# A fused decoder block on one core: the identity products of two rounds taken out of TensorE's order

## The reference, cut to what matters

```python
x = x + L0_attn(layernorm(x), ...)          # gated delta rule: per head a 16 x 16 state,
                                            #   Sd = g * S;  S = Sd + k (beta * (v - k Sd));  o = q S
x = x + L0_xattn(layernorm(x), ctx, ctx)    # differential cross attention over 64 context rows
x = x + L0_ffn(layernorm(x), ...)           # causal convolution, 8 experts (top 2), small GELU block
```

## Time and profile before

| | us |
|---|---|
| three runs, median | 1509.95 |
| lowest, highest | 1508.57, 1512.37 |
| the profiled execution | 1508.25 |
| its span, first to last instruction | 1506.5 |

### The profile page before, as it was taken

How to read it: one execution, slowest core, us unless ns; L and a number is a source line. 1 busy time by engine, 2 the same in 40 slices (tenths; PEclk the granted TensorE clock), 3 DMA queues, 4 the chain that set the end, 5 groups by cost and what they waited for, 6 DMA issues and landing times.

```text
span 1506.5 us, 38146 instructions
## 1 busy us (share of the span) xinstructions
PE 1429.3 (95%) x15790; PEld 945.8 (63%) x15790; DVE 1187.0 (79%) x3205; ACT 834.3 (55%) x1599; POOL 205.5 (14%) x212
## 2 busy tenths in 40 slices
PE   5988899999999999999999999999999989899899
PEld 3654666655766566656766567655766557756765
DVE  7457978978887878977897888977898778966663
ACT  2555365646655565655756566655656455534453
POOL 0121211102301022002301023002201022001000
PEclk7999999999999999999999999999999999999999
DMA  6010010000100001000100001000100001000000
GB/s 236 1 29 30 2 29 22 10 1 15 30 29 2 2 18 26 30 2 2 43 30 2 2 15 29 30 1 2 44 15 3 1 16 30 16 2 15 1 1 15
DMA packets 20212, 31.27 MB, mean 21 GB/s; under 512 B 1480, under 2 KB 17864, under 8 KB 19784
## 3 DMA queue, kind: packets, MB, share of 16 engines
q1 hardware_dynamic: 20040, 28.82, 6.6%
HBM read 20.41 MB, written 8.39 MB: 19 GB/s over the span
## 4 chain that ended last, share of the span: by engine, by line
PE 80%; DVE 11%; ACT 6%; issue 2%; POOL 0%; DVEq 0%; ACTq 0%
PE bank L2116 15%; PE bank L2054 7%; PE bank L1808 7%; PE bank L1678 6%; PE four L1899 4%; PE bank L2039 4%; PE bank L2017 4%; PE bank L1703 3%; PE bank L1811 3%; PE four L1967 3%; PE four L1951 2%; PE four L1703 2%; PE bank L1684 2%; PE bank L1710 2%; PE four L1918 2%
## 5 line engine op out<-in xcount | busy, mean ns | idle before, releaser
L2116 PE MATMUL bank<-w_sb,cs 128*128 128x512 f32 x512 | 245.2, 597 | 0.3 <-ACT cs L1032 0.3
L739 POOL TENSOR_TENSOR decayed<-state,pk 128x512 f32<-128x512 f32 x64 | 67.7, 1058 | 842.0 <-DVE state L1414 842.0
L2116 PEld LDWEIGHTS bank<-w_sb,cs 128*128 128x128 f32 x512 | 94.6, 190 | 91.2 <-issue 83.4
L1032 ACT ACTIVATE cs<-bank 128x512 f32<-128x512 f32 x112 | 66.7, 595 | 148.8 <-PE bank L1684 126.2
L2054 PEld LDWEIGHTS bank<-vx_sb,cs 128*128 128x128 f32 x896 | 109.2, 190 | 25.9 <-ACT cs L982 16.6
L2054 PE MATMUL bank<-vx_sb,cs 128*128 128x136 f32 x896 | 119.9, 285 | 3.6 <-ACT cs L982 1.5
L982 ACT COPY cs<-bank 128x512 f32<-128x512 f32 x114 | 66.5, 583 | 95.3 <-PE bank L2039 95.3
L1808 PE MATMUL bank<-hT,w_sb 128*128 128x512 f32 (+1 forms) x224 | 109.4, 611 | 2.7 <-ACT rota L835 0.8
L1626 DVE SCALAR_TENSOR_TENSOR cs<-cs,rwt 128x256 f32<-128x256 f32 x196 | 88.7, 501 | 23.5 <-ACT cs L1032 22.4
L1273 DVE SCALAR_TENSOR_TENSOR qkv<-pre,l_sb,qkv 128x512 f32<-128x512 f32 x144 | 99.4, 746 | 0.2
L1498 DVE TENSOR_REDUCE pkc<-bank 128x8 f32<-128x512 f32 x116 | 75.0, 681 | 20.3 <-PE bank L2017 20.3
(11 more groups left out here) (283 smaller groups left out, 3015.7 us busy)
## 6 DMA issues: line engine op xcount, KB each, us to landing
xt<-in_x SPq DMA_DIRECT2D x8, 512.0 KB, 4.8
vscr<-qkv SPq DMA_DIRECT2D x8, 512.0 KB, 2.6
vT<-vscr SPq DMA_DIRECT2D x32, 128.0 KB, 4.4
Tm<-in_x SPq DMA_DIRECT2D x8, 512.0 KB, 3.8
out<-cs SPq DMA_DIRECT2D x8, 512.0 KB, 2.9
w_sb<-in_weights SPq DMA_DIRECT2D x1, 3656.0 KB, 18.1
w_sb<-in_weights SPq DMA_DIRECT2D x1, 1456.0 KB, 8.3
cs<-in_scratch SPq DMA_DIRECT2D x3, 256.0 KB, 8.6
```

The source lines that it names most:

```text
L2116: mm(dst, x1T[:, k, b * TB:b * TB + TB], ew[:, k, ep * 512:ep * 512 + 512], start=k == 0, stop=False)
```

## The change

The entries of KEEP for round 0 and for round NI - 1 are deleted: 51 products of round 0 and 44 of round 7, 95 of the 235. With the number 0, keep issues nothing and waits for nothing. Every other product of this kind stays, and so do all other instructions of all five engines, in the same order. The table's text gets six lines shorter, so that a line of the changed kernel has a number lower by six than the same line before.

```diff
-        20): 2, (-1, -1, "moe", 21): 6, (-1, -1, "moe", 3): 6, (-1, -1, "moe", 7): 1, (-1, 0, "co", 4, 0): 9,
-        (-1, 0, "cs", 4, 1): 1, (-1, 0, "raw", 2): 6, (-1, 1, "db"): 2, (0, -1, "moe", 19): 2, (0, -1, "moe",
-        22): 6, (0, -1, "moe", 30): 1, (0, -1, "sc", 6, 0): 8, (0, -1, "turn5", 1): 10, (0, 0, "co", 4, 1): 2,
-        (0, 0, "vturn"): 11, (0, 1, "proj", 1, 0): 1, (0, 2, "turn1", 0): 5, (0, 2, "turn1", 1): 5, (1, 0, "co",
-        1, 1): 3, (1, 0, "z", 3): 9, (NI - 1, -1, "pt", 5): 5, (NI - 1, -1, "pt", 6): 2, (NI - 1, -1, "pt", 7):
-        3, (NI - 1, -1, "pt", 9): 3, (NI - 1, -1, "pv", 1, 0): 3, (NI - 1, -1, "pv", 4, 0): 3, (NI - 1, -1,
-        "turn3", 1): 3, (NI - 1, 0, "co", 3, 0): 1, (NI - 1, 0, "co", 5, 1): 1, (NI - 1, 0, "sum", 2): 5, (NI -
-        1, 0, "wo", 1): 14, (NI - 1, 1, "gate", 1): 1, (NI, -1, "moe", 3): 1, (NI, -1, "pw", 0, 0): 17, (NI, -1,
-        "pw", 0, 1): 1, (NI, -1, "sc", 1, 0): 4, (NI, -1, "turn2", 0): 1, (NI, 0, "cs", 5, 1): 8, (NI, 0, "d1",
-        5): 9, (NI, 0, "decay"): 17, (-2, -1, "ffd", 1): 23, (-2, -1, "moe", 28): 3, (-2, -1, "pt", 6): 3, (-2,
-        -1, "pw", 0, 0): 7, (-2, -1, "sc", 1, 0): 11, (-2, -1, "turn6", 0): 4, (-2, 0, "co", 4, 1): 7, (-2, 0,
-        "cs", 6, 1): 6, (-2, 0, "raw", 1): 5, (-2, 2, "turn1", 0): 16}
+        20): 2, (-1, -1, "moe", 21): 6, (-1, -1, "moe", 3): 6, (-1, -1, "moe", 7): 1, (-1, 0, "co", 4, 0): 9, (-1, 0,
+        "cs", 4, 1): 1, (-1, 0, "raw", 2): 6, (-1, 1, "db"): 2, (1, 0, "co", 1, 1): 3, (1, 0, "z", 3): 9, (NI, -1,
+        "moe", 3): 1, (NI, -1, "pw", 0, 0): 17, (NI, -1, "pw", 0, 1): 1, (NI, -1, "sc", 1, 0): 4, (NI, -1, "turn2", 0):
+        1, (NI, 0, "cs", 5, 1): 8, (NI, 0, "d1", 5): 9, (NI, 0, "decay"): 17, (-2, -1, "ffd", 1): 23, (-2, -1, "moe",
+        28): 3, (-2, -1, "pt", 6): 3, (-2, -1, "pw", 0, 0): 7, (-2, -1, "sc", 1, 0): 11, (-2, -1, "turn6", 0): 4, (-2,
+        0, "co", 4, 1): 7, (-2, 0, "cs", 6, 1): 6, (-2, 0, "raw", 1): 5, (-2, 2, "turn1", 0): 16}
```

## The result

| | before | changed |
|---|---|---|
| median of 6 runs each, us | 1508.05 | 1522.61 |
| lowest, highest | 1504.37, 1512.37 | 1520.27, 1526.71 |
| the profiled execution | 1508.25 | 1520.27 |
| its span | 1506.5 | 1518.4 |
| its mean granted clock | 0.991 | 0.976 |

The changed kernel takes 1.0087 times as long, 95% interval 1.0065 to 1.011, 13.1 us more by the ratio (the plain medians are 14.6 apart). The forecast was slower by 5.8 us, 1515.8 with a range of 1509 to 1521. The sign is right; the size is less than half of what was measured, and the median lies 1.6 us above the range.

What follows compares the result with a forecast made beforehand. PE looked like the bound at 95% busy, but other engines pace the removed groups, so TensorE's clock decides. Clock-fall terms sum to 8.9 us; 0.7 of that, 6.2, less 0.4 gained gives +5.8: 1515.8 us, range 1509 to 1521.

Steps and rivals of the forecast that it cites:

- The 95 products give nothing back: Both rounds: of 21.2 us of PE time removed, only 0.4 us is gained, since other engines set the pace.
- in the way: Rival: a third of 64 exposed products delay the step behind them, so removal gains 4.8 us, 1505.2; chance 0.06.
- 96 to 100: Round 0: a clock fall slows vturn and cond behind it, 0.6 us (0 to 1.7).
- 119 to 123: Round 0: a clock fall slows the next projection, with ACT right behind it, 1.3 us (0 to 1.7).
- 167 to 182: End of round 0: two more falls behind the one at 171, mostly hidden by DVE, 1.0 us (0 to 3.4).
- Three pairs of pt and pv: Round 7 (1268, 1275, 1282): a fall doubles pv, whose DVE reader follows; 1.3 each, 3.9 us (0 to 5.1).
- behind other work: Rival: the clock falls, but DVE has other work first, so only +2.2 us, 1512.2; chance 0.14.
- The thinner groups at 1233, 1263, 1315: Round 7: falls at these smaller groups cost 0.4 us together (0 to 3.4).
- Ahead of wo: Round 7: a fall doubles part of wo's 3.68 us and DVE waits, 1.7 us (0 to 1.7).
- wo's 16 records still take less than 4 us: Round 7, sign that the forecast is wrong; it expected about 5.4 us instead of 3.7.
- taking 0.7 of it: Whole sum: 8.9 us cut to 6.2 for stretches where the clock holds, as at 1221.
- rival of the standing PE: Only gaps leaving PE idle over 3 us, ahead of vturn and wo, lose the clock: +1.9 us, 1511.9; chance 0.18.

Runs made afterwards that it cites:

- e11: Kernel before without 11 products of round 7 (turn3, co, sum, gate): 1513.31 us against 1508.83, 1.0024.
- e5: Kernel before without the 31 products at the end of round 0: 1511.84 us, ratio 1.0016, not told from no change.
- e6: Kernel before without the first 20 products of round 0: 1511.46 us, ratio 1.0006, not told from no change.
- e8: Kernel before without the 14 products ahead of wo in round 7: 1511.38 us, ratio 1.0013, not told from no change.
- e9: The changed kernel itself measured again, all 95 products gone: 1520.34 us against 1508.83 for the kernel before, 1.0082.
- e2: Kernel before without the 44 products of round 7, those of round 0 kept: 1520.68 us against 1508.46, 1.0087.
- e10: Kernel before without the 44 products of round 7, measured once more in a later set: 1517.93 us against 1508.83, 1.0069.
- e3: Kernel before with all 95 products kept, but on a 32 x 32 part of the array in rounds 0 and 7: 1528.49 us against 1508.46, 1.0134.
- e1: Kernel before without the 51 products of round 0, those of round 7 kept: 1516.56 us against 1508.46, 1.0056.

## Why the prediction was right, and where it wasn't

- **The 95 products give nothing back** (0.4 us of 21.2): right. Ahead of btr the distance moves by -0.20, as said. Ahead of wo it moves by -0.03. The rival "in the way" falls.
- **96 to 100**, 0.6: measured +0.8, from -0.97 at 82 us to -0.20 at 105. Right.
- **119 to 123**, 1.3: the distance goes from -0.40 to +1.19 between 122 and 136, +1.6. Right, at its upper end.
- **167 to 182**, 1.0: +2.4. The prediction expected "two more behind it" with DVE ahead for most of it; a single fall lasts 3.4 us. What came is one stretch of 20.5 us, which lasts into the end of the round, where PE's steps are on the path.
- **Three pairs of pt and pv**, 3.9, at most 5.1: +1.2, +2.3 and +1.6, together 5.1, the upper bound. The second fall lasts 6.8 us instead of 3.4. DVE waits for each pv, so the rival "behind other work" falls here; it held for a part of round 0, where 17 us more of half speed cost 2.4 us.
- **The thinner groups at 1233, 1263, 1315**, 0.4: +3.2 at 1313 to 1331 alone, a stretch of 10.2 us. In relation to its size this is the worst-sized term: it was put near zero without a reason, and taking these 11 products out alone costs 4.5 us in the medians (e11). How much of the 3.2 is the products' is open, since the same place lost 4.2 to 4.3 us in e5, e6 and e8 with all of them in.
- **Ahead of wo**, 1.7, the only term put at its upper bound: 0 in this execution and in e9, 1.5 in the traces of e2, e8 and e10. PE stands still there in all five, so standing still does not always lose the clock. The prediction had named "wo's 16 records still take less than 4 us" as a sign of being wrong; they take 3.72 us, and for this term it was.
- **What none of the terms had:** +1.7 at 1229.5, ahead of wo in round 6, which the change doesn't touch, and -1.3 for the fall at 444 that only the trace before has.

The step that failed is the amount of half speed: **"taking 0.7 of it"**, and the terms that counted one fall, or two, where the clock then stayed down. Behind the first 40 us there are nine separate half-speed stretches instead of three; six more lie within the "five to eight" of the prediction, but it did not foresee how long they last. The bounds of the terms, 17.0 at 1.7 each, hold ten falls, each seen as an event of 3.4 us that ends by itself; their sum of 8.9 is 0.89 for a fall. That mean price was about right: 0.89 / 3.4 is 0.26 us per us at half speed, where the runs with at least 20 us more at half speed show 0.16 (e5) to 0.39 (e2). But ten falls times 0.7 are 24 us at half speed, and the profile has 47.7 us more than before, the medians 50. 50 / 3.4 = 14.7 falls at 0.89 are 13.1 us, near the measured 13.1 to 14.6; that it fits so well is luck, since the 0.89 is a mean over terms that were too low and one that was too high.

The factor alone isn't all of it: without it the forecast would have been 8.9 - 0.4 = +8.5 us, 1518.4, inside the range. The terms themselves measured 0.8 + 1.6 + 2.4 + 5.1 + 3.2 + 0 = 13.1 in the trace instead of 8.9, and the differences lie in the thinner groups (+2.8), the end of round 0 (+1.4), the pairs (+1.2) and wo (-1.7). The factor was taken from the one gap at 1221 that kept the clock, ahead of wo in round 6; the same gap lost it in most of the later traces.

The "rival of the standing PE" gave 1511.9. The Trainium skill, in "TensorE: Matmul & The Clock Gate", section "What's actually happening", tells the clock's fall as that of an idle array. These traces agree where PE stood and the clock fell (ahead of vturn and, at times, of wo), and disagree in the pairs of round 7, where PE's longest idle time was 0.77 us with the products and without, and above all in e3, where the clock fell with PE busy for 5.00 of 5 us and stayed at half speed with PE busy for 26.52 of 27.

**What stays open.** The parts don't add to the whole: e5 and e6 give 0.0016 and 0.0006 against 0.0034 and 0.0056 for both together in two sets of runs, and e1 and e2 add up to more than the change in both sets. The intervals of the single parts are about ±0.2%, and the untouched weak places lose the clock in some kernels and not in others, so no cause can be put on the difference. Why two more sets of fills gained nothing is open too. No run measures how much of e3's +20 us is overrun alone; its trace has 6.6 us more than the changed kernel's at the end of round 0, but it is the trace of the longest of its four runs. Why the clock falls in one execution and not in the next at wo and from 1313 to 1334 no run here shows.

## What to carry to other kernels

A product that computes nothing can be worth keeping: judge it not by the gap that it fills but by the granted clock of the stretch when it's gone. When such products go, price the time at half speed, not a number of falls, because a clock that is down can stay down: here for up to 20.5 us behind which small products and short waits stood. Where a kernel's own runs scatter with their mean clock, as here 1503.8 to 1517.0, read the slope from them before the change is priced, and read parts that are worth less than that scatter from the places of the falls in several traces: a dozen runs each didn't tell 2 to 3 us from nothing here.

## What the runs showed of the hardware

- Busy is not enough. PE busy for 26.52 us of 27, half of it with products on a quarter of the array's rows and columns, was granted 0.50 (e3), and PE busy for 6.61 of 7 us was granted no more at the end of round 0 of the changed kernel. The clock also fell, from 1.00 to 0.50, with PE busy for 5.00 of the 5 us before, 2.27 of them with such products (e3, ahead of wo).
- PE's idle time doesn't decide alone: the clock held behind 2.92 us of it ahead of wo in the changed kernel, and fell in the pairs of round 7, where the longest was 0.77 us.
- A low clock can last: 20.5 us in one stretch (171.4 to 191.9), 10.2 us in another (1321.7 to 1331.9), where the kernel before had three of 3.4 us each behind its first 40 us.
- One microsecond at half speed costs this kernel 0.41 us, a little less than the 0.46 of four projection records ((3.68 - 1.98) / 3.68), and nearly the same slope, 0.40, is found in three other sets of its runs.
- The clock of an unchanged kernel differs from run to run, 0.984 to 0.994, and with it the time by 13 us, as much as the whole effect of the change.
